# One sine product over a reversed view of the halves, and one sum of squares for q and k, in an attention and feed-forward kernel

## The reference

```python
h = shift_token(x)
q, k, v = jnp.split(h @ wqkv, 3, axis=-1)        # 8 heads of 64
q = l2norm(q) * qs
k = l2norm(k) * ksc
# rotary_xpos:
q = q * cos * scale + rotate_half(q) * sin * scale
k = k * cos / scale + rotate_half(k) * sin / scale
# rotate_half(x) = concatenate([-x2, x1]) of the two halves x1, x2 of a head
```

## Time and profile before

| | |
|---|---|
| median of three executions | 452.82 us (451.48 to 452.88) |
| span of the profiled execution | 452.5 us |
| median less that span | 0.3 us |
| busy: PE, PEld, DVE | 391.6, 258.5, 342.2 us |
| busy: ACT, POOL | 299.5, 205.4 us |
| steps of the two pipelines | about 75 to 225 us and 257 to 415 us |

### The profile page before, as it was taken

One profiled execution on the slowest core, in us unless ns is written; L12 is line 12 of the kernel. 1 busy time (PEld: TensorE's weight loads), 2 busy tenths in 40 slices (PEclk: granted clock), 3 DMA queues, 4 the chain that ended last, 5 costly groups with the idle time before them and its releaser, 6 DMA issues.

```text
span 452.5 us, 8032 instructions
## 1 busy us (share of the span) xinstructions
PE 391.6 (87%) x2504; PEld 258.5 (57%) x2504; DVE 342.2 (76%) x1308; ACT 299.5 (66%) x986; POOL 205.4 (45%) x229
## 2 busy tenths in 40 slices
PE   0678677799999999987789888999999999867995
PEld 0456552477777767765434345767767777654442
DVE  2688747899999999984135689999999999612345
ACT  2355533589899899886432338889898998653224
POOL 6261103585775766762000066767757757410000
PEclk9988985999999999999989989999999999967898
DMA  7920000000000000000000000000000000000003
GB/s 158 292 55 2 1 1 0 0 3 1 1 2 2 0 2 1 3 0 1 0 1 0 1 0 2 0 3 2 2 0 1 3 1 1 2 1 0 0 0 93
DMA packets 10263, 7.25 MB, mean 16 GB/s; under 512 B 3245, under 2 KB 9431, under 8 KB 10222
## 3 DMA queue, kind: packets, MB, share of 16 engines
q1 hardware_dynamic: 8590, 5.63, 4.6%
q0 software_dynamic: 832, 1.12, 1.3%
q10 hardware_dynamic: 800, 0.00, 0.1%
HBM read 5.70 MB, written 1.05 MB: 15 GB/s over the span
## 4 chain that ended last, share of the span: by engine, by line
DVE 56%; PE 31%; issue 6%; ACT 4%; DMA 1%; SPq 0%; DVEq 0%; ACTq 0%
DVE pp L986 11%; PE ps L511 10%; DVE shared L971 8%; DVE ss L978 8%; DVE shared L968 7%; PE ps L618 5%; DVE kT L997 4%; PE ps L386 3%; DVE vv L1001 3%; DVE xs L1008 2%; PE ps L566 2%; PE ps L535 1%; DVE pri L993 1%; DVE nm L986 1%; DVE shared L872 1%
## 5 line engine op out<-in xcount | busy, mean ns | idle before, releaser
L386 PE MATMUL ps<-wqkv_raw,xs 128*128 128x512 f32 x192 | 108.2, 652 | 11.1 <-DVE shared L971 11.1
L340 POOL TENSOR_TENSOR pp<-pp,pri 128x512 f32<-128x512 f32 x64 | 66.6, 1041 | 94.8 <-DVE pri L993 94.8
L757 ACT ACTIVATE pp<-pp,nm 128x128 f32<-128x128 f32 x256 | 99.2, 389 | 10.3 <-DVE nm L986 10.3
L347 POOL TENSOR_TENSOR shared<-shared 128x512 f32<-128x512 f32 x64 | 81.4, 1275 | 0.0
L986 DVE CUSTOM_DVE_ANT_0 pp<-ps,msk,rr 128x128 f32<-128x128 f32 x256 | 72.4, 347 | 0.0
L511 PE MATMUL ps<-hn,w1g 128*128 128x512 f32 (+1 forms) x96 | 49.4, 637 | 5.8 <-DVE uu L1063 5.8
L757 ACT ACTIVATION_READ_ACCUMULATOR pp<-pp,nm 128x1 f32 x256 | 48.1, 188 | 0.0
L971 DVE TENSOR_TENSOR shared<-ps,stab 128x256 f32<-128x256 f32 x128 | 47.6, 413 | 0.0
L386 PEld LDWEIGHTS ps<-wqkv_raw,xs 128*128 128x128 f32 x192 | 31.1, 200 | 27.0 <-DVE shared L971 17.7
L968 DVE TENSOR_TENSOR shared<-ps,ctab 128x512 f32<-128x512 f32 x64 | 42.9, 671 | 2.5 <-ACT sqr L668 2.4
L559 PEld LDWEIGHTS ps<-pT,vv 128*64 128x64 f32 x512 | 28.2, 139 | 26.9 <-issue 24.1
(11 more groups left out here) (118 smaller groups left out, 673.1 us busy)
## 6 DMA issues: line engine op xcount, KB each, us to landing
wqkv_raw<-in_L_ffn_wqkv_dram SPq DMA_DIRECT2D x1, 1536.0 KB, 16.4
out_dram<-shared SPq DMA_DIRECT2D x4, 256.0 KB, 2.5
w_raw<-in_L_ffn_w_dram SPq DMA_DIRECT2D x1, 682.0 KB
xt<-in_x_dram SPq DMA_DIRECT2D x2, 256.0 KB, 4.5
xt<-in_x_dram SPq DMA_DIRECT2D x1, 512.0 KB, 12.4
wo_raw<-in_L_ffn_wo_dram SPq DMA_DIRECT2D x1, 512.0 KB
ct<-in_ctx_dram POOLq DMA_DIRECT2D x1, 360.0 KB, 12.2
w_raw<-in_L_ffn_w_dram SPq DMA_DIRECT2D x2, 128.0 KB
```

The lines of the kernel that those rows point to most:

```text
L340: T(pp[m.j][:, a, :, :], pp[m.j][:, a, :, :], pri[m.j][:, a * 4:a * 4 + 4].unsqueeze(2).to_broadcast([128, PAIRS, 128]), ALU.mult).then_in ...
L347: T(cs[m.j][:, part], cs[m.j][:, part], sn[m.j][:, part], ALU.add).then_inc((aq_done, ak_done)[s], 1)
L386: mm(ps[:, part, :], xs[:, m.b, 0:N], wqkv_raw[:, m.layer, part * INNER:(part + 1) * INNER], start=True, stop=True).then_inc((q_ps, k_ps, ...
L757: A(pp[m.j][:, a, c, :], pp[m.j][:, a, c, :], ACT.Exp, bias=nm[m.j][:, a * 4 + c:a * 4 + c + 1], scale=-1.0, accum_out=psum_[m.j][:, a * 4 ...
```

## The change

Two functions of the vector block and one wait of POOL are rewritten.

`turns` made the sine product in two instructions per q or k, each over 32 of the 64 columns of the eight heads. It now makes one over all 512 columns: the PSUM operand is viewed as (head, half, column) with the halves in reverse order, the result and the table in plain order. `squared` made one sum for q and one for k; it now makes one over both, 128x16 from 128x1024, and waits for both squares ahead of it. `sq_sum` is raised once per batch instead of twice, so `clamped` waits for half the count.

```diff
             def clamped(m):
 
-                pool.wait_ge(sq_sum, 2 * m.i + 2)
+                pool.wait_ge(sq_sum, m.i + 1)
                 nc.gpsimd.tensor_scalar(ssc[m.j][:], ss[m.j][:], 1e-24, None, ALU.max).then_inc(ss_ready, 1)
...
                 V.tensor_tensor(heads(cs[m.j], s), x_, ctab[:, m.layer, s, :].unsqueeze(1).to_broadcast([128, HEADS, DH]), ALU.mult)
-                for u in range(2):
-                    o_, i_ = slice(u * 32, u * 32 + 32), slice(32 - u * 32, 64 - u * 32)
-                    last = V.tensor_tensor(heads(sn[m.j], s)[:, :, o_], x_[:, :, i_],
-                                           stab[:, m.layer, s, o_].unsqueeze(1).to_broadcast([128, HEADS, 32]), ALU.mult)
-                last.then_inc(done, 1)
-
-            def squared(m, s):
-
-                dve.wait_ge((sqq_done, sqk_done)[s], m.i + 1)
-                V.tensor_reduce(ss[m.j][:, s * HEADS:(s + 1) * HEADS], heads(sqr[m.j], s), AX.X, ALU.add).then_inc(sq_sum, 1)
+                turned = ps[:, QB + s, :].rearrange("p (h u e) -> p h u e", u=2, e=32)[:, :, ::-1, :]
+                V.tensor_tensor(sn[m.j][:, s * INNER:(s + 1) * INNER].rearrange("p (h u e) -> p h u e", u=2, e=32), turned,
+                                stab[:, m.layer, s, :].rearrange("p (u e) -> p u e", u=2).unsqueeze(1).to_broadcast([128, HEADS, 2, 32]),
+                                ALU.mult).then_inc(done, 1)
+
+            def squared(m):
+
+                dve.wait_ge(sqq_done, m.i + 1)
+                dve.wait_ge(sqk_done, m.i + 1)
+                V.tensor_reduce(ss[m.j][:], sqr[m.j][:].rearrange("p (h d) -> p h d", d=DH), AX.X, ALU.add).then_inc(sq_sum, 1)
...
                 if on(3):
-                    squared(at(3), 0)
-                    squared(at(3), 1)
+                    squared(at(3))
```

## The result

The changed kernel takes 449.32 us in the median of five executions (448.88 to 449.79), against 452.47 for five of the kernel before taken with it: a ratio of 0.9931, 95% interval 0.9909 to 0.9952. That is 3.1 us, and the forecast was 1.0. Medians in this text are over all executions of a run; ratios and intervals leave out those that took over 1.5% more than the fastest of the same kernel.

A forecast was written before the change was run, and what follows sets the result against it. A loop of PE and ACT, 8.32 us a step, was taken as the bound, covering DVE's saving; 0.80 (fills) + 0.15 (stalls) + 0.05 (steady steps) = 1.0 us turned 452.8 into 451.8 us, range 450.4 to 453.3.

The forecast's parts named there:

- Rival A: Steady steps: DVE is the bound and its saving of 0.23 us in 26 steps passes through; 446.0 us, chance 0.12.
- the tie: At project_q: DVE's release by q's sine product comes just in time for PE; an earlier one gains only some thousandths.
- Sine product: DVE's sine products for q and k: each merge saves 0.08 us of queue; q's end comes after 0.67 instead of 0.75.
- Sum: DVE's sums of squares: merging two, which take 1.19 us, into one saves 0.07 us of queue a step.
- DVE's busy time: Whole profile after: forecast to fall by some 7 us to about 335.
- Rival B: Sine products: the reversed view is read more slowly and the kernel becomes slower, 454.1 to 478 us; chance 0.07.
- the sum: Whole kernel: 0.80 from the fills, 0.15 from late memsets and 0.05 from steady steps make 1.0 us.
- the stalls: Two steps where DVE reached the memset late for "issue", 0.43 us instead of 0.07; 0.08 back from each, 0.15.
- The fills: While each layer's pipeline fills, DVE decides: 0.64 from sine products and 0.21 from sums, 0.80 us taken.
- the eight waits: PE idle until a sine product was done, four times in each layer's fill; each saves 0.08, together 0.64 us.
- The change, part by part: Part of the prediction that prices sine products, sums of squares and what reaches the end, from one profiled execution of 452.5 us.
- The range's low bound: Whole kernel: each term at its top, 1.74 plus 0.72 for the stalls, is 2.4 us, so 450.4.

The follow-up runs named there:

- e13: Kernel before plus two one-column memsets on DVE ahead of q's turns in the twelve full steps of each layer; 454.68 us, one run.
- e14: Changed kernel plus two one-column memsets on DVE ahead of q's turns in the twelve full steps of each layer; 445.39 us, one run.
- e15: Changed kernel with project_q of one batch in the second layer made twice (0.86 us more PE work), repeated for twelve executions; 454.52 us.
- e7: Changed kernel with project_q of one batch in the second layer made twice (0.86 us more PE work), six executions; 446.44 us.

## Why the prediction was wrong

**The bound was read rightly.** Steady steps of 8.32 us before and after, waits of DVE in place of its work, PE's busy time complete, the chain now on PE: each as named. Rival A, that DVE's saving passes through, is out; 0.23 us in 26 steps isn't found in any step, and e13 and e14 show the tie from both sides. The Trainium skill ("Perfetto Trace Analysis", Identifying the Most-Contended Engine) would have named DVE by occupancy; the trace disagrees: DVE lost 96 instructions and no steady step became shorter. One thing the reading passed over: PE's weight load L571 also waits for DVE, 0.24 us a step for L1008 (122.85 us before, 123.07 after). It delays no matmul, since `project_q` runs meanwhile. That the kernel got faster by over 0.3% doesn't bear rival A out.

**The terms.** Sine product: 0.75 to 0.68 us for its end, forecast 0.67. Sum: 1.19 to 1.13 us of queue (119.89 to 121.02), 0.06 saved, 0.07 forecast. DVE's busy time fell by 4.1 us (342.2 to 338.1), where 7 were forecast. Rival B is out at 681 ns. From the clock's rise near 81 us to the last `out_proj` but one the profiles give 317.29 - 316.43 = 0.86 us, and the executions 0.9 ± 0.3 at equal clock, where the sum said 1.0. Within the 0.86 the stalls gave more than forecast: distances between scores of 8.67 us twice and 8.37 twice before, and of 8.56 twice after, against 8.32, so 0.32 less, forecast 0.15. The fills gave less, about 0.5 for the six of the eight waits that lie behind the rise.

**The step that failed** is at the head of "The change, part by part", where all durations are taken from one profiled execution and the same 0.3 us is put around them before and after. The sum so took every duration at the clock of the profile before. The half-clock time, 46.9 us of an average execution, stood in it with a change of nothing and without a reason, and no rival asked whether it would stay. It fell by 9.8 us, to 37.1, worth 2.9 us. The profile had what would have raised the question: the row of the granted clock in 40 slices, of the kernel before and then after.

```profile
PEclk9988985999999999999989989999999999967898
```

```profile
PEclk9968985899999999999989989999999999999999
```

Before, the second layer's drain stands at six and seven tenths (slices 36 and 37) and the first layer's at nine, for the same instructions. The second drain is where the two profiles part: from the start of `out_proj` of batch 14 to the end it is 54.45 us before and 49.96 after. The range's low bound, 450.4, had room for sizes and stalls, and none for this.

The 9.8 us of half clock at 0.30 are 2.9 us, which with the 0.9 at equal clock is 3.8, the difference between the means of all executions; the first ten gave 3.1. The 2.9 come mostly from the drains: filling them brings both kernels to the same half-clock time. They came because the change moved the second drain against the raster, not because fewer instructions were left. With 0.86 us of PE work beside it, the same change had a median 2.0 us above the kernel before in e15 and 5.9 below it in e7.

**What stays open.** How much half-clock time single executions of one kernel have in the cross attention and the first fill differs (four intervals ahead of 81 us in some profiles, two ahead of 75 in others), and what sets it was not tried. Why the clock near 262 us falls in some executions wasn't either. The places on the raster at which it fell or stayed come from one profile of each kernel, and why it falls at 0.1 to 0.5 us and at 1.8 to 2.3, and not between, is open.

## What to carry to other kernels

Where two engines are both full, compare each wait's distance with the distance where that wait is real: it tells who sets the pace, and it held here to 0.01 us (0.15 and 0.03, before and after). But a forecast below one per cent also needs the row of the granted clock: find holes of PE that stand beside a fall of it, ask how a shift of the work by some tenths would change it, and put its price into the range. And before a gain of this size is ascribed to an edit, take it at equal clock, or fill the hole in both kernels; 1.9 us of spare matmuls a layer (1.16 + 0.71) took 5 us from the kernel before, more than the edit did.

## What the hardware showed that I had not expected

- The time of one and the same kernel follows its mean granted clock, 0.30 us for each us of half clock, from 450.4 us (0.957) to 456.6 (0.940).
- The clock's changes lie on a raster of 3.41 us, and whether it falls in a hole of 1.1 us of PE depends on where the hole stands on it: 0, 1.72, 2.58 and 3.44 us of added work gave 452.8, 450.4, 451.3 and 456.1 us, and the clock stayed in all 19 unfilled drains with the instant 0.71 to 1.68 us behind the start of `out_proj`.
- A product whose PSUM operand is read with its halves in reversed order takes 681 ns for 512 columns, against 672 in plain order (both in the profile after).
- Two one-column memsets behind each other took 0.04 us of DVE's queue together (e13), as much as the one ahead of the scores takes alone (125.27 to 125.31 there).
